# A state-space layer with routed experts: combination on GpSimd, first states on ScalarE, three bank sets for the last quads, and a new order of pieces

## What is computed

```
u, z  = conv(in_proj_x(ln(x))), in_proj_z(ln(x))           # 256 channels each
dt    = clip(sigmoid(u @ dt_w.T + dt_b), 1e-4, 1)
B, C  = u @ B_w.T, u @ C_w.T                                # 16 states each
state[n] = exp(dt * A[n]) * state[n] + dt * u * B[n] + 1e-6 # over 256 steps
y     = sum_n state[n] * C[n] + D * u
x1    = x + (y * silu(z)) @ out_w.T
t     = ln(x1)
shared = (silu(t @ sg.T) * (t @ su.T)) @ sd.T
w     = top 2 of sigmoid(t @ router.T + bias), divided by their sum   # 8 experts
routed = sum_e w[e] * ((silu(t @ wg[e].T) * (t @ wu[e].T)) @ wd[e].T)
out   = x1 + shared + routed
```

## Time and profile before

| | us |
|---|---|
| median of three executions (lowest, highest) | 1439.51 (1438.04, 1442.42) |
| profiled execution, its own time | 1441.34 |
| profiled execution, span from first to last instruction | 1439.6 |
| busy in the span: TensorE, VectorE, ScalarE, GpSimd | 1240.6, 1221.1, 893.8, 791.7 |
| first scan starts, last pair of scans ends | 44.9, 1303.9 |
| mean granted TensorE clock, as a share of 2.4 GHz | 0.970 |

### The profile page before, as it was taken

How to read it: one execution, slowest core, us unless ns; L and a number is a source line. 1 busy time by engine, 2 the same in 40 slices (tenths; PEclk the granted TensorE clock), 3 DMA queues, 4 the chain that set the end, 5 groups by cost and what they waited for, 6 DMA issues and landing times.

```text
span 1439.6 us, 27184 instructions
## 1 busy us (share of the span) xinstructions
PE 1240.6 (86%) x8709; PEld 1023.9 (71%) x8709; DVE 1221.1 (85%) x2396; ACT 893.8 (62%) x1399; POOL 791.7 (55%) x1318
## 2 busy tenths in 40 slices
PE   6788897899889898998989898998989898887883
PEld 3566666587777787786768777777777677776873
DVE  0699999898898989899998989999898989995331
ACT  2774757476776766666865766766765757752221
POOL 3445453854377553856467553866557553773342
PEclk9799999999999999999999999999999999998997
DMA  5000000032324143133423142133324142246873
GB/s 173 1 1 8 2 8 5 30 115 63 107 84 127 39 127 114 54 98 96 118 80 125 39 133 90 59 118 96 118 71 132 34 132 63 77 144 184 263 234 114
DMA packets 110655, 132.30 MB, mean 92 GB/s; under 512 B 10032, under 2 KB 81584, under 8 KB 110384
## 3 DMA queue, kind: packets, MB, share of 16 engines
q1 hardware_dynamic: 102320, 113.73, 25.6%
q0 software_dynamic: 8192, 16.79, 4.0%
HBM read 102.37 MB, written 28.11 MB: 91 GB/s over the span
## 4 chain that ended last, share of the span: by engine, by line
DVE 38%; PE 33%; issue 13%; ACT 9%; POOL 4%; DMA 2%; DVEq 0%; SPq 0%; POOLq 0%; ACTq 0%
DVE h L1070 17%; DVE yT L1088 12%; PE p_misc L908 6%; PE p_hT L876 5%; PE p_db L862 4%; PE p_dn L1015 4%; PE p_gu L1003 3%; PE p_misc L919 3%; ACT dA L740 2%; PE p_misc L902 2%; PE p_gu L995 2%; PE p_misc L945 1%; DVE x L1216 1%; POOL ysel L679 1%; POOL xs_dram L665 1%
## 5 line engine op out<-in xcount | busy, mean ns | idle before, releaser
L1070 DVE TENSOR_TENSOR_SCAN h<-dA,p_db 128x512 f32<-128x512 f32 x512 | 598.8, 1203 | 76.4 <-PE p_db L862 49.0
L632 POOL TENSOR_SCALAR dBT<-wT,bcT 128x256 f32<-128x256 f32 x704 | 338.6, 481 | 373.0 <-ACT wT L769 204.8
L1088 DVE SCALAR_TENSOR_TENSOR yT<-p_hT,bcT,yT 128x256 f32<-128x256 f32 x960 | 396.9, 471 | 9.4 <-PE p_hT L876 9.4
L862 PE MATMUL p_db<-ident,dBT 128*128 128x128 f32 x2048 | 297.3, 278 | 82.8 <-DVE h L1070 70.0
L862 PEld LDWEIGHTS p_db<-ident,dBT 128*128 128x128 f32 x2048 | 233.8, 142 | 145.6 <-issue 121.3
L740 ACT ACTIVATE dA<-dt_sb,A_sb 128x510 f32<-128x510 f32 x512 | 329.7, 709 | 5.4 <-DVE h L1070 4.7
L876 PE MATMUL p_hT<-ident,h 128*128 128x128 f32 x2048 | 292.7, 280 | 25.7 <-DVE yT L1088 16.5
L876 PEld LDWEIGHTS p_hT<-ident,h 128*128 128x128 f32 x2048 | 231.6, 143 | 68.4 <-DVE yT L1088 36.6
L679 POOL DMA_INDIRECT ysel<-ys_dram,slot x128 | 123.4, 964 | 97.3 <-DVE x L1216 38.4
L795 ACT ACTIVATE dBT<-wT,eps,bcT 128x256 f32<-128x256 f32 x320 | 163.5, 587 | 7.6 <-PE p_db L862 7.6
L665 POOL DMA_INDIRECT xs_dram<-xn,slot x128 | 126.8, 990 | 56.6 <-issue 36.0
(11 more groups left out here) (115 smaller groups left out, 1374.3 us busy)
## 6 DMA issues: line engine op xcount, KB each, us to landing
wring<-w_moe_dram SPq DMA_DIRECT2D x191, 384.0 KB, 4.3
xt<-xs_dram SPq DMA_DIRECT2D x41, 256.0 KB, 4.8
ys_dram<-yo SPq DMA_DIRECT2D x41, 256.0 KB, 2.3
x_sb<-x_dram SPq DMA_DIRECT2D x16, 256.0 KB, 4.3
out_dram<-x SPq DMA_DIRECT2D x16, 256.0 KB, 2.6
xs_dram<-ysel SPq DMA_DIRECT2D x4, 512.0 KB, 5.5
xs_dram<-xn,slot POOLq DMA_INDIRECT x128, 2.3
ysel<-ys_dram,slot POOLq DMA_INDIRECT x128
```

Source lines behind the costliest of these rows:

```text
L632: op = pool.tensor_scalar(dBT[:, j % DBT_RING, c], wT[:, g % 2, c], bcT[:, g % 2, c, n:n + 1], STATE_EPS, ALU.mult, ALU.add)
L862: mm = pe.transpose(p_db[half][:, c * P:(c + 1) * P], dBT[:, j % DBT_RING, c, half * P:(half + 1) * P], ident[:])
L1070: dve.tensor_tensor_scan(h[:, j % 2, half], dA[:, j % DA_RING, half], p_db[half][:], 0.0, ALU.mult, ALU.add).then_inc(scan_done, 1)
L1088: op = dve.scalar_tensor_tensor(yT[:, g % 2, cc], p_hT[pair][:, c], scalar, yT[:, g % 2, cc], ALU.mult, ALU.add)
```

## The change

1. **GpSimd combines.** For the groups 0 to 11 a new `add_routed` on GpSimd multiplies all of `ysel` (128x1024) by the shares in one instruction and adds its two halves (128x512 each) to `x1`. The last four groups stay on VectorE (`COMB_DVE = 4`).
2. **First state on ScalarE.** `multiply_state` (`m0`, `m1`: two activations of 128x256 each) takes the place of line 1086 (`BY_ACT = 1`). The transposes of the unit behind, and the first sums on VectorE, wait for it. `add_more` has nothing to do at `BY_ACT = 1`.
3. **The end.** From slot 257 a quad comes every slot and takes the next of three sets of banks: `p_gu`, `p_db` or `p_hT`, the latter two free once the scans and sums are done. The space of `dA` holds eight more weight tiles. From slot 236 on quads come every two slots. The last scatters come earlier, two to a slot.
4. **Order and distances.** All five tables have a new order, `EXP_LEAD` is 4 instead of 3 and `ROUTE_RING` 5 instead of 3.

```diff
+BY_ACT = 1
+COMB_DVE = 4
-EXP_LEAD = 3
+EXP_LEAD = 4
-ROUTE_RING = 3
+ROUTE_RING = 5
...
 PE_SLOTS = (
-    "U h N G i0 i1 X", "h yb0 i0 i1 G U N yb1", "h X U i0 i1 G xnT N", "h u0 N U i0 i1 G X X",
-    "h op U N i0 G i1 X", "h U u1 G i0 i1 N", "h xn2T G U i0 dt0 i1 X N X", "h dt1 N U i0 i1 G logit X",
+    "U h N i0 G i1 X", "h U yb0 i0 N i1 yb1 G", "X h U i0 xnT i1 N G", "h u0 N U i0 i1 X X U",
+    "N h G i0 op i1 X", "U G h u1 i0 G N h i1", "U X xn2T i0 G i1 dt0 X", "N h dt1 N U i0 i1 logit X G",
...
 DVE_SLOTS = (
-    "stats1 s0 s1 y0 y1", "P Q s0 C s1 y0 y1 yd0 P Q", "s0 s1 yd1 Q y0 y1 C", "s0 s1 C y0 y1 C P Q P",
+    "stats1 s0 s1 y0 P y1", "C Q s0 s1 Q P yd0 y0", "s0 s1 yd1 y1 Q C y0 y1", "s0 C C y0 s1 P y1 P Q",
...
 ACT_SLOTS = (
-    "V d x x X", "x V E d d X", "x V d xnT E", "x V E X", "d u0 X x X u1 E E V", "d x d x V X", "E xn2T X V",
-    "d dt0 dt1 E d V x X sig", "x E V X", "E x d bc d V X", "E x V z0 z1 d", "x d E X X V", "E d d x X V",
+    "x x d V x m0 d X", "E m1 V d", "x X xnT d V", "E x E X V d", "u0 X x E X E u1 V d", "x d V x E X",
+    "xn2T V X", "dt0 E d d dt1 sig x V X", "E x X d V", "E x d bc E V", "x V z0 z1 d E X",
...
 POOL_SLOTS = (
-    "", "c S d d c ln1", "gate0 c d S c", "S gate1 d c c", "d S S d", "ln2 S", "",
-    "c c S S d d d d c c clip c S c S", "", "", "d d S S", "c c w0 w1 S", "", "d S c d", "", "c d d S S")
+    "", "d d c c S d c c C C ln1", "", "d C c d gate0 gate1 c C S S", "d C S S", "C c ln2 c C d d d C S", "",
+    "c c c c S d clip S C S d C d C S", "", "", "c c w0 w1 C S d S", "C", "", "c d S C c d S", "",
+    "d C C S S")
...
 POOL_LAST = (
-  "gate0 gate1 S", "ln2 S", "S", "S", "S", "S", "S", "S", "S", "S", "S", "S", "S", "S", "S", "S")
+    "gate0 gate1", "", "", "", "", "", "", "", "", "", "", "", "", "", "",
+    "ln2 C S C S C S C S C S C S C S C S C S C S C S C S C S C S C S C S")
 SP_LAST = (
...
+    "O T W T W O O T", "", "T W Y", "O T Y W Y Y", "T W O", "O T O W Y W W", "", "O T O Y T Y", "W O",
+    "Y T W T", "T O Y O W", "W Y", "W T O O Y T", "O", "T Y Y W Y W W T O Y Y", "")
...
-LAST_SCATTER = 6
+LAST_SCATTER = 3
-FAST_SLOTS = 12
-FAST_FROM = NS * GROUPS - FAST_SLOTS
-FAST_QUAD = 2
+TAIL = NS * GROUPS + 1
+TAIL_QUAD = 1
+TAIL_WEIGHT = 3
+END_SLOTS = 20
+END_FROM = NS * GROUPS - END_SLOTS
+END_QUAD = 2
...
+def bank_sets():
+    sets, before, last = [], [], {}
+    for at, (slot, _) in enumerate(ORDER):
+        chosen = 0 if slot < TAIL else (sets[-1] + 1) % 3
+        sets.append(chosen)
+        before.append(last.get(chosen))
+        last[chosen] = at
+    return sets, before
...
+            def add_routed(g, j):
+                b, m = place_of(g)
+                if j == 0:
+                    pool.wait_ge(ysel_loaded, 128 * (g + 1))
+                    pool.wait_ge(dn_emptied, QUAD["shared", g] + 1)
+                    shares = weight[:, b % ROUTE_RING, :, CHUNKS * m:CHUNKS * (m + 1)]
+                    pool.tensor_tensor(ysel[:], ysel[:], shares.rearrange("p j (c o) -> p j c o", o=1).broadcast_to(
+                        [P, 2, CHUNKS, DM]), ALU.mult).then_inc(comb_scaled, 1)
+                    pool.wait_ge(comb_scaled, g + 1)
+                else:
+                    pool.wait_ge(comb_done, 2 * g + 1)
+                pool.tensor_tensor(x1[:, g % X1_RING], x1[:, g % X1_RING], ysel[:, j], ALU.add).then_inc(comb_done, 1)
...
+            def multiply_state(g, n, pair):
...
+                act.wait_ge(hT_in_psum, PAIRS * j + pair + 1)
...
+                for c in range(2):
+                    cc = 2 * pair + c
+                    into = yT[:, g % 2, cc] if n == 0 else y_more[:, cc]
+                    op = act.activation(into, p_hT[pair][:, c], ACT.Copy, scale=bcT[:, g % 2, cc, NS + n:NS + n + 1])
+                op.then_inc(mul_done, 1)
...
                 pe.wait_ge(scan_done, 2 * j + 2)
                 for pair in range(PAIRS):
-                    at_least(pe, mac_done, PAIRS * (j - 1) + pair + 1)
+                    if j and (j - 1) % NS < BY_ACT:
+                        pe.wait_ge(mul_done, sums_before(j - 1, pair, True))
+                    elif j:
+                        pe.wait_ge(mac_done, sums_before(j - 1, pair, False))
```

More of the change, by code:

```diff
@@ L34 @@
 DT_MIN = 1e-4
-BATCHES = tuple((g, g + 1) for g in range(0, GROUPS - 2, 2)) + ((GROUPS - 2,), (GROUPS - 1,))
+ALONE = 2
+BATCHES = tuple((g, g + 1) for g in range(0, GROUPS - ALONE, 2)) + tuple((g,) for g in range(GROUPS - ALONE, GROUPS))
 MOST = max(len(gs) for gs in BATCHES) * CHUNKS
@@ L284 @@
 XT0 = tuple(sum(-(-r // 4) for r in ROUTED[:b]) for b in range(len(BATCHES)))
+TAIL_TILE = ROUTED0[-2]
+SPARE = 8
 def quad_of_routed(at):
@@ L296, in routed_quad, with sums_before @@
     return b, at - XT0[b]
+def sums_before(j, pair, by_act):
+    if j < 0:
+        return 0
+    full, n = divmod(j, NS)
+    if by_act:
+        return PAIRS * (full * BY_ACT + min(n, BY_ACT)) + (pair + 1 if n < BY_ACT else 0)
+    return PAIRS * (full * (NS - BY_ACT) + max(0, n - BY_ACT)) + (pair + 1 if n >= BY_ACT else 0)
 def of_kind(kind, j):
@@ L414, in build, with weights_of @@
         p_misc = pb("p_misc", [P, TOK])
+        spare = dA[:].rearrange("p n h t -> p (n h t)").rearrange("p (n f) -> p n f", f=WROW)
+        def weights_of(at):
+            if at < TAIL_TILE:
+                return wring[:, at % W_RING], w_loaded[at % W_RING], 16 * (at // W_RING + 1)
+            turn, place = divmod(at - TAIL_TILE, W_RING + SPARE)
+            if place >= W_RING:
+                return spare[:, place - W_RING], spare_loaded[place - W_RING], 16 * (turn + 1)
+            place = (TAIL_TILE + place) % W_RING
+            return wring[:, place], w_loaded[place], 16 * (len(range(place, TAIL_TILE, W_RING)) + turn + 1)
+        gu_banks = [p_gu, [p_db[i][:].rearrange("p (f t) -> p f t", f=2) for i in range(2)], p_hT]
+        hm_of = [hm[:]] + [wT[:, j].rearrange("p (i f) t -> p i f t", f=2) for j in range(2)]
         tap_weights = sem("tap_weights")
@@ L461, in build @@
         w_loaded = [sem(f"w_loaded{j}") for j in range(W_RING)]
+        spare_loaded = [sem(f"spare_loaded{j}") for j in range(SPARE)]
         gate_in_psum = sem("gate_in_psum")
@@ L704, in _ @@
                         weigh_u(ahead, int(name[1]))
+                    if name in ("m0", "m1") and u - NS * k < BY_ACT - 1:
+                        add_more(group_of(k, 0), u - NS * k + 1, int(name[1]))
                     if name in ("gate0", "gate1") and behind is not None:
                         gate(behind, int(name[4]))
+                    if name == "C":
+                        for g, j in due.get(("comb", u), ()):
+                            if g < GROUPS - COMB_DVE:
+                                add_routed(g, j)
                     if name == "S":
@@ L807, in silu @@
                 at = QUAD[quad]
-                at_least(act, down_in_psum, at)
+                into, banks = hm_of[BANK_SET[at]], gu_banks[BANK_SET[at]]
+                if BEFORE[at] is not None:
+                    act.wait_ge(down_in_psum, BEFORE[at] + 1)
+                elif BANK_SET[at]:
+                    act.wait_ge(scan_done, HALVES * UNITS)
                 for i in range(2):
```

143 lines of the change are left out of this document (91 added, 52 removed), and 20 rows, old and new, of tables (ACT_SLOTS, DVE_LAST, DVE_SLOTS, PE_SLOTS).

## The result

The changed kernel takes 1421.0 us (median of four; 1419.7 to 1425.9). The kernel before took 1438.8 us in the same session: a ratio of 0.987, 95% interval 0.985 to 0.989, or 17.8 us less. The forecast was 43 us less. The profiled execution has a span of 1424.1 us against 1439.6, and it is 4.9 us above its own median (profiled time 1425.9), so that 15.5 of the 17.8 us can be followed in the two traces.

What follows compares the result with a forecast made beforehand. TensorE was taken to bound slots 2 to 8 of a group, VectorE slots 9 to 1. Steady part 31 plus end 12 gave 43 us off the profiled 1441.3: 1398.3, or 1396.5 for the median; range 1366 to 1422.

Steps and rivals of the forecast that it cites:

- the sum of the steady part: Groups 0 to 15: 3.3, 24.6 and 3 us gained, together 31 us; bounds 5 and 58.
- which leaves 3: Group 15: VectorE's net 4.0 us gain cut to 3, as TensorE takes on 1.3 quads and reaches 74 us.
- 0.5 for `m1`: Each group: `m1` ends about when the next unit's `h` wants its bank; charged 0.5 us (0 to 1.2).
- 0.2 for the order: Each group: one more half-quad piece in slots 3 to 8, against fewer ScalarE table loads; 0.2 us lost.
- the end: After the last scan: the 10.7 us wait for stores goes, routing gains nothing; 123.8 us instead of 135.7, 12 less.
- The combination: Line 1216 to GpSimd, twelve groups: 2.3 us saved in every second group, nothing in slots 4 and 5; 1.15 a group.
- The first state: Line 1086, slot 1, to ScalarE: VectorE saves 1.6 us a group, 1.1 net.
- The means: Steady part taken at 78.6 us a group, over 16 groups between the first scan and the end of the last.
- Rival 1: TensorE's half swallows VectorE's savings, the order brings no more: steady part 5, end 12, 1422.5 us; chance 0.12.
- The signs: What would show it: middle group 76 to 77 us, `p_db` waits 40 us or more, last scan ending about 1273.
- Rival 4: GpSimd's queue holds clamps and `dBT` behind the combination in seven groups; at 8 us each 1452.5 us; chance 0.06.
- Rival 5: VectorE and GpSimd exclude each other: one routing step in eight batches held 2.5 us, 20 us, 1416.5; chance 0.04.

Runs made afterwards that it cites:

- e1: The changed kernel with all combinations back on VectorE: 1427.5 us, 0.991 of before.
- g3: The changed kernel with ScalarE's `m1` directly behind `m0`, the state input behind them: 1420.2 us, 0.985 of before.
- e3: The changed kernel with ScalarE emptying the bank of the convolution's first half ahead of the state input (`dBT`): 1418.8 us, 0.984 of before.
- h1: The changed kernel with e3's edit, and GpSimd's layer norm and one `dBT` ahead of the combination: 1408.2 us, 0.977 of before.
- h4: The edits of h1 and g4 together on the changed kernel: 1385.2 us, 0.960 of before.
- g4: The changed kernel with two of the convolution's four taps left out, so TensorE has less work: 1406.7 us, 0.975 of before.
- e2: The changed kernel with the first state's product back on VectorE, in the new order: 1463.7 us, 1.016 of before.
- g1: The changed kernel with group 11 combined on VectorE too (`COMB_DVE = 5`): 1415.7 us, 0.982 of before.
- f2: As f1, plus the first state's product on ScalarE: 1460.0 us, 1.012 of the kernel before.
- e4: The changed kernel with quads coming every two slots only in the last twelve slots, as before: 1440.8 us, 1.001 of before.
- f1: The kernel before with the new end alone; combination and first state on VectorE, old order: 1446.6 us, 1.004 of before.
- g2: The changed kernel with SyncE's load of quad (7,0) ahead of group 11's outputs: 1417.3 us, 0.983 of before.
- f3: As f1, plus the combination of groups 0 to 11 on GpSimd: 1463.2 us, 1.015 of the kernel before.

## Why the prediction was right in direction and wrong in size

**The step that failed** is the sum of the steady part, as the prediction put it: "Groups 3 to 14: 12 x (1.1 + 1.15 - 0.2) = 24.6", and "which leaves 3" for group 15. It took what VectorE sheds, less 0.5 for `m1` and 0.2 for the order, as what every group gains. Only the odd groups gained it. The steady part was to give 31 us and gave 1.5, of 17.1 in the odd groups and a loss of 15.6 in the others. The terms, in spans:

| term | forecast | measured |
|---|---|---|
| groups 0 to 2 | -3.3 | +3.5 |
| odd groups 5 to 13 (1.1 + 2.3 - 0.2 each) | -16.0 | -17.1 |
| group 3 | -3.2 | +2.2 |
| even groups 4 to 14 (1.1 - 0.2 each) | -5.4 | +1.0 |
| group 15 | -3.0 | +8.9 |
| the end | -11.9 | -15.2 |
| start | 0 | +1.0 |

- **The combination, right.** 2.3 us in every second group was forecast; e1 measured 2.2 in odd groups and nothing in even ones, for the reason given: there it lies in slots 4 and 5, where VectorE waits anyway. The count of groups was off, though. Line 1216 first runs at 483.8 us, in group 5, so group 3 had no combination to lose (2.3 of its 3.2), and of the two put down to group 15 the second starts at 1305 us, behind the last scan.
- **The first state, right in unit 1, mis-sized in what it leads to.** Nearly all of the 1.6 us came in unit 1 (4.44 to 2.88 us in groups 4 to 14). I charged 0.5 for `m1`. In odd groups units 2 to 8 take 0.2 less than before, in even groups 1.8 more. g3 shows that `m1`'s place is not the reason. The charge belonged to the order (e3 and h1 find the wait at unit 4 in ScalarE's table), which I had put at 0.2 a group from a count of pieces by slot. The count cannot see the wait at unit 4, since that depends on who stands ahead of whom in ScalarE's queue.
- **The means, wrong.** I reasoned with 78.6 us a group, a mean that takes in the short first groups; the steady groups were 84.4 and 79.3, and an even group had 6.4 us of VectorE's idle time, an odd one 6.1. The window from 752 to 831 us in the earlier trace rows straddles two groups, and so hid the difference, and the two half-group windows of the earlier trace rows lie in one even group but for their last 7 us, so that they say nothing of the odd ones.
- **Rival 1** gave 1422.5 us, within 2 us of what was measured, but not by its mechanism. Of the 3.8 us that VectorE shed in an even group, two waits in series had swallowed 1.9 (h1). TensorE's work counts only once these are gone (h4 against g4); what holds the other 1.9 is open. The sum of rival 1, 5 in the steady part and 12 at the end, was met by luck: the steady part gave 1.5 and the end 15.2.
- **Group 0.** It took 69.0 us against 64.0, and group 3 74.5 against 72.3. Over the runs in the new order these two come in pairs, 68.9 and 74.4 us or 67.0 and 72.8, by no edit that would explain it (two runs with half the convolution and e2 are left out here). The granted clock goes with the pair: from 25 to 50 us after group 3's first scan it is 0.86 in the changed kernel and 0.93 in g1, and from 14 to 30 us after group 0's 0.92 and 1.00. The changed kernel's profiled execution has the long pair, 3.6 us of its 4.9 above the median if the median execution has the short one, which no trace shows. So group 3 lost 0.5 to 2.2 us and group 0 3 to 5. In its first 14 us TensorE was busy 9.0 us at a granted clock of 0.62, where the kernel before had 11.7 of 15 us at 0.82. TensorE waits in the group 2.8 us for ScalarE's products, which is new; the 4.2 us for GpSimd's `dBT` it also waited before. In the old order the first state on ScalarE costs group 0 2.2 us (f2, 65.8 against 63.6). What the rest comes from was not taken apart.
- **Group 15.** TensorE took on 74 matmuls (584 against 510), 1.5 quads of 48, near the forecast 1.3, and its busy time rose to 73.3 us as forecast (74). But that its idle time would fill the difference, "which leaves 3", was wrong: it stayed at 12.3 us, and the group grew by about as much as TensorE's busy time (8.8 us). The mean granted clock fell from 1.00 to 0.94 there, with e4 at 1.00 and as long (86.5, with 604 matmuls), so the clock is not the main cause. That the added quads are, no run shows: none has the new order and fewer of them in group 15. In f1, with the old order, the group takes 105.2 us, so the order matters by 20. Which of its new waits (2.7 us for a product, 2.5 us for `both_hits`, 2.2 us of VectorE for a down product) are needed was not settled, so the cause of this term stays open.
- **The end, right by most of its own steps.** Forecast and measured after the last scan, in us: last routing step L + 44 and L + 42.1, group 12's gathers L + 55.4 and L + 52.7, group 15's L + 107.3 and L + 104.0, end L + 123.8 and L + 120.5:
```profile
1330.01 0.40 SPq L606 DMA_DIRECT2D out_dram<-x  x1
1330.52 1.04 SPq L591 DMA_DIRECT2D xt<-xs_dram  x2
...
1342.14 0.19 PE L1058 MATMUL p_misc<-both_hits,tri 128*128 128x32 bf16 x1 [0.69 <-ACT xT L877]
...
1345.46 0.16 DVE L1325 TENSOR_SCALAR expert_of<-expert_f 1x15 int32<-1x15 f32 x1
...
1345.91 1.10 POOL L740 DMA_INDIRECT xs_dram<-xn,slot  x1 [15.93 <-DMA ys_dram<-yo]
...
1356.16 0.99 POOL L754 DMA_INDIRECT ysel<-ys_dram,slot  x1 [0.30 <-issue]
...
1372.49 0.94 POOL L754 DMA_INDIRECT ysel<-ys_dram,slot  x1 [6.57 <-DVE x L1350]
...
1392.33 0.94 POOL L754 DMA_INDIRECT ysel<-ys_dram,slot  x1 [10.16 <-DVE x L1350]
...
1407.53 0.94 POOL L754 DMA_INDIRECT ysel<-ys_dram,slot  x1 [5.51 <-DMA ys_dram<-yo]
```
  The output, the load behind it, `rank` and the eight scatters stand in the order that was worked out, and g1 and g2 show that the links are real. The last wait, for a store, is 5.5 us against 18.8; I had named such a wait as a sign of being wrong. It cost little, since the three cycles before it took 51.3 us against 51.9. That the three bank sets are what took the long wait off, as the prediction has it, no run shows by itself (e4).
- **The signs.** The last scan ended at 1303.5 us and not at about 1273, `p_db` kept VectorE waiting 36 us and not 40 or more, and there is no middle group of 76 to 77 us: the odd ones took 75.9, the even ones 84.4.
- **Rival 4** did not come in the changed kernel, but f3 shows it at 3 us an even group in the old order. **Rival 5** came in one place at a size that counts, below.

## What to carry to other kernels

Price a piece not by a period's mean but by the group and the slot it leaves, and measure the periods of the groups one by one first: two kinds of group may have two bounds. If a stretch does not answer to less work on either busy engine, look for short pieces (a copy that empties a bank, a norm) queued behind one that waits for a DMA or behind a longer one; here two such waits hid each other, so take all of them away in one run before giving up. When work is moved to another engine, move the order with it: the same three moves were worth -18 us with a new order and +30 with the old.
